# A recurrent mixer and a gated FFN, tile by tile: the FFN's pieces moved to other places in the order, with alternating PSUM banks

## What is computed

```python
xx  = x_prev - x
mix = tanh((x + xx * maa_x) @ maa_w1)          # five mixes of 32: w, k, v, r, g
mw, mk, mv, mr, mg = einsum(mix, maa_w2)
xw, xk, xv, xr, xg = x + xx * (maa_{w,k,v,r,g} + m{w,k,v,r,g})
r, k, v, g = xr @ Wr.T, xk @ Wk.T, xv @ Wv.T, silu(xg @ Wg.T)
decay = exp(-exp(time_decay + tanh(xw @ td_w1) @ td_w2))
# scan over time, state S of 16 heads, 32 x 32 each
y_t = r_t @ (S + u * k_t v_t);   S = decay_t * S + k_t v_t
y = groupnorm(y) * ln_g + ln_b
x1 = layernorm(x + (y * g) @ Wo.T)
h  = gelu(x1 @ ternary(W_fc).T)                # 2048 wide
out = layernorm(x1 + layernorm(h) @ ternary(W_proj).T)
```

## Time and profile before

| what | value |
|---|---|
| median of 3 runs | 3530.97 us |
| the runs | 3509.68, 3533.42 and 3530.97 us |
| the profiled execution | 3509.35 us, of which the span is 3507.2 us and 2.15 us lie around it |
| mean granted TensorE clock in it | 0.983 |
| PE busy | 3143.1 us (90%) |
| DVE busy | 2473.1 us (71%) |
| ACT busy | 1897.2 us (54%) |
| POOL busy | 784.9 us (22%) |

### The profile page before, as it was taken

How to read it: one execution, slowest core, us unless ns; L and a number is a source line. 1 busy time by engine, 2 the same in 40 slices (tenths; PEclk the granted TensorE clock), 3 DMA queues, 4 the chain that set the end, 5 groups by cost and what they waited for, 6 DMA issues and landing times.

```text
span 3507.2 us, 98753 instructions
## 1 busy us (share of the span) xinstructions
PE 3143.1 (90%) x39261; PEld 2257.9 (64%) x39261; DVE 2473.1 (71%) x5108; ACT 1897.2 (54%) x3852; POOL 784.9 (22%) x725
## 2 busy tenths in 40 slices
PE   1899999999999999999999999999999999999997
PEld 0566666766666766666666666766666766666764
DVE  8466686776676676776766776676786776677776
ACT  0445556645566555566555566555566655556653
POOL 3122211122221122221222221222211122221121
PEclk9899999999999999999999999999999999999998
DMA  4000000000000000000000000000000000000000
GB/s 184 14 8 19 20 14 17 17 14 20 14 17 20 17 14 20 14 17 20 17 14 20 14 17 20 17 14 20 14 19 18 17 20 14 20 14 17 20 17 13
DMA packets 22598, 73.04 MB, mean 21 GB/s; under 512 B 3041, under 2 KB 3297, under 8 KB 20545
## 3 DMA queue, kind: packets, MB, share of 16 engines
q1 hardware_dynamic: 22208, 66.76, 5.4%
HBM read 49.97 MB, written 16.78 MB: 19 GB/s over the span
## 4 chain that ended last, share of the span: by engine, by line
PE 25%; DVE 22%; issue 21%; ACT 19%; POOL 10%; POOLq 1%; DMA 1%; ACTq 1%; DVEq 0%; SPq 0%
PE psP L393 7%; ACT ARENA L653 7%; PE psP L423 6%; ACT HHI L810 6%; POOL MT L856 5%; POOL ARENA L870 4%; PE psF L615 4%; ACT GG L801 3%; DVE ARENA L1125 3%; DVE ARENA L1087 3%; DVE ARENA L1077 2%; DVE HLO L1237 2%; DVE SUMS L1229 2%; DVE GR L1245 2%; PE psX L375 1%
## 5 line engine op out<-in xcount | busy, mean ns | idle before, releaser
L393 PE MATMUL psP<-ARENA,WALL 128*128 128x256 f32 x3072 | 692.0, 382 | 0.2 <-ACT ARENA L684 0.2
L653 ACT ACTIVATE ARENA<-ARENA 32x512 f32<-32x512 f32 (+1 forms) x992 | 578.8, 583 | 189.8 <-DVE ARENA L1077 137.7
L393 PEld LDWEIGHTS psP<-ARENA,WALL 128*128 128x128 f32 x3072 | 574.6, 190 | 84.5 <-issue 11.3
L1237 DVE SCALAR_TENSOR_TENSOR HLO<-GG,FWB,HHI 128x128 f16<-128x128 f32 x1024 | 292.3, 347 | 459.8 <-ACT HHI L810 455.7
L615 PE MATMUL psF<-XHI,WFC 128*128 128x128 f16 x4096 | 490.0, 220 | 46.5 <-DVE XLO L1216 34.0
L615 PE MATMUL psF<-XLO,WFC 128*128 128x128 f16 x4096 | 488.8, 220 | 0.0
L615 PEld LDWEIGHTS psF<-XHI,WFC 128*128 128x128 f16 x4096 | 401.7, 99 | 88.1 <-issue 86.0
L615 PEld LDWEIGHTS psF<-XLO,WFC 128*128 128x128 f16 x4096 | 402.9, 98 | 14.0 <-issue 10.3
L870 POOL TENSOR_TENSOR ARENA<-ARENA,XT 128x1024 f32<-128x1024 f32 x128 | 285.2, 2228 | 507.4 <-DVE ARENA L1029 507.4
L634 PE MATMUL psF<-WPJ,HHI 128*128 128x512 f16 x1024 | 389.8, 381 | 3.1 <-ACT GG L801 3.1
L634 PE MATMUL psF<-WPJ,HLO 128*128 128x512 f16 x1024 | 388.1, 379 | 0.0
(11 more groups left out here) (166 smaller groups left out, 5418.0 us busy)
## 6 DMA issues: line engine op xcount, KB each, us to landing
XT<-x_ch SPq DMA_DIRECT2D x33, 520.0 KB, 3.4
ARENA<-x_tok SPq DMA_DIRECT2D x32, 512.0 KB, 4.1
out<-OUT SPq DMA_DIRECT2D x64, 256.0 KB, 2.0
WALL<-w_all SPq DMA_DIRECT2D x5, 1024.0 KB, 16.6
ARENA<-wfc SPq DMA_DIRECT2D x4, 1024.0 KB, 7.9
ARENA<-wpj SPq DMA_DIRECT2D x3, 1024.0 KB, 14.6
GG<-wpj SPq DMA_DIRECT2D x1, 1024.0 KB, 18.6
OUT<-w2a SPq DMA_DIRECT2D x8, 64.0 KB, 14.9
```

Of the source, the lines that this page charges most:

```text
L393: mm = pe.matmul(psP[:, P.bank(f"{name}{g}"), COLS * c:COLS * (c + 1)], WALL[:, w, k, 128 * (2 * g + c):128 * (2 * g + c + 1)], cc(XF[slot ...
L653: return act.activation(o, i, ACT.Copy)
L1237: e = dve.scalar_tensor_tensor(out=HLO[:, k, :], in0=GG[:, u % 2, 0, 128 * m:128 * (m + 1)], scalar=FWB[:, 0, k:k + 1], in1=HHI[:, k, :], ...
```

## The change

Computation and instruction counts stay the same but for four things: each fold of the sums is two TENSOR_REDUCEs of half the size, one SCALAR_TENSOR_TENSOR of 128x1 becomes a TENSOR_SCALAR (the FFN's variance), the names of `XF[0]` and `XF[1]` are swapped for the mixes (so the decay's input no longer shares the gated output's buffer), and the banks of psF follow a table. All else is order:

- VectorE: the last FFN piece `up(1, 3)`, the fold of its sums and `stored` of the first pair go behind the gated output. `late` is cut into `moments` (behind mix "mk"), `product`, `late_normed` and `late_stored`, with mixes and `up(0, 0)` between them. The decay's mix goes behind the first half of the output product. Level 2's right scaling goes in front of `up(0, 3)`, and the first pair's fold goes behind the merges of levels 4 and 8.
- TensorE: mix "mw" between `wo0` and `wo1`; `down(1, 3)` from the body's end to behind td1 of the next body.
- ACT: tanh of the gate's second half behind the second level's query copies. POOL and SP: the late roots and the late store follow VectorE's new order; the same DMAs are issued in the same order.

```diff
+F_BANKS = [0, 1, 0, 1, 0, 1, 1, 0, 1, 0, 1, 0]
 class Ring:
     def bank(self, name):
-        return self.names.index(name) % self.depth
+        return self.banks[self.names.index(name)]
     def wait_free(self, eng, it, name, first):
-        i = self.names.index(name) - self.depth
+        own = self.names.index(name)
+        i = next(i for i in range(own - 1, own - 1 - self.n, -1) if self.banks[i % self.n] == self.banks[own])
...
@@ TensorE
                 mm.then_inc(p_full, 1)
+                if ffn:
+                    ffn.late()
                 mix(it - 1, 2, "mv", wait_free)
...
                     mm.then_inc(p_full, 1)
+                    if p == 0:
+                        mix(it, 0, "mw", wait_free)
                 if ffn:
                     ffn.stats(1)
-                mix(it, 0, "mw", wait_free)
-                if ffn:
-                    ffn.down(1, 3)
...
+                def late():
+                    if not first:
+                        down(before, 1, 3)
@@ ACT
-                    if i == 0:
-                        if ffn:
-                            ffn.up(0, 3)
+                    if i == 0 and ffn:
+                        ffn.up(0, 3)
+                    if i == 1:
                         gate(1)
@@ POOL
-                    v = XF[f % 2].rearrange("p (q t) -> p q t", t=CH)
+                    v = XF[(f + 1) % 2].rearrange("p (q t) -> p q t", t=CH)
                     pool.tensor_tensor(v, v, xcur, ALU.add).then_inc(xf_ready, 1)
-                    if f == 2 and ffn:
+                    if f == 1 and ffn:
                         ffn.late()
...
+                        if ffn:
+                            ffn.late_normed()
@@ VectorE
                 mix(it, 1, "mk", None)
                 if ffn:
+                    ffn.moments()
                     ffn.normalise()
...
                 mix(it, 3, "mr", "k1")
                 if ffn:
+                    ffn.late_normed()
                     ffn.up(0, 0)
+                    ffn.late_stored()
...
                 if ffn:
                     ffn.up(0, 2)
+                scale_right(1, 2)
+                if ffn:
                     ffn.up(0, 3)
                 for i, n in enumerate(LEVELS):
-                    scale(i + 1, n)
+                    if i:
+                        scale_right(i + 1, n)
+                    scale_left(i + 1, n)
...
                     dve.wait_ge(w_dve, W.read(it, f"l{n}"))
-                scale(5, 32, ffn.fold if ffn else None)
+                    if ffn and n in (4, 8):
+                        ffn.fold(0, n // 4 - 1)
+                scale(5, 32)
...
-                if ffn:
-                    ffn.up(1, 3)
-                    ffn.stored()
                 dve.wait_ge(y_copied, 2 * it + 2)
...
                 dve.tensor_tensor(YSB[:, 512:1024], YSB[:, 512:1024], G[:, 512:1024], ALU.mult).then_inc(z_ready, 1)
                 if ffn:
-                    ffn.stats(1)
+                    ffn.up(1, 3)
+                    ffn.fold(1, 0)
+                    ffn.fold(1, 1)
+                    ffn.stored()
...
                     dve.bn_stats(BNS[:, p, :], X1[:, p, :]).then_inc(bn_done, 1)
-                decay_input(it, "wo1")
+                    if p == 0:
+                        decay_input(it)
...
+                def fold(p, i):
+                    dve.wait_ge(sums_added, 3 * (PAIRS * j + p) + 3)
+                    dve.tensor_reduce(GR[:, i, :], SUMS[:, i, :].rearrange("p (m t) -> p t m", m=4), AX.X, ALU.add).then_inc(sums_folded, 1)
```

More of the change, by code:

```diff
@@ L67, in __init__ @@
         self.before = before
+        self.banks = banks or [i % depth for i in range(self.n)]
         assert self.n % depth == 0
     def bank(self, name):
-        return self.names.index(name) % self.depth
+        return self.banks[self.names.index(name)]
     def full(self, it, name):
@@ L91, with __init__ @@
 class FeedForward:
-    def __init__(self, alone, normalise=None, tokens=None, up=None, stats=None, down=None, bias=None, finish=None, normed=None, stored=None, fold=None, late=None):
+    def __init__(self, alone, normalise=None, tokens=None, up=None, stats=None, down=None, bias=None, finish=None, normed=None, stored=None, fold=None, moments=None, late_normed=None, late_stored=None, late=None):
         self.alone, self.tokens, self.up, self.stats, self.down = alone, tokens, up, stats, down
@@ L233, in rwkv_ffn_kernel @@
         X = Ring(X_SEQ, 1, x_full, {"act": x_act, "dve": x_dve})
-        F = Ring(F_SEQ, 2, f_full, {"act": f_act, "stats": f_stats, "product": f_product})
+        F = Ring(F_SEQ, 2, f_full, {"act": f_act, "stats": f_stats, "product": f_product}, banks=F_BANKS)
         xprev, xcur = XT[:, :, 0:CH], XT[:, :, 1:CH + 1]
@@ L638, in alone @@
                 def alone():
+                    late()
                     tokens()
@@ L643, in alone @@
                         for part in range(4):
-                            down(p, part)
+                            down(j, p, part)
                         stats(p)
-                return FeedForward(tokens=tokens, up=up, stats=stats, down=down, alone=alone)
+                def late():
+                    if not first:
+                        down(before, 1, 3)
+                return FeedForward(tokens=tokens, up=up, stats=stats, down=lambda p, part: down(j, p, part), late=late, alone=alone)
             over_tiles(pe, tile, feed_forward)
@@ L923, in late, with late_normed @@
                         scale_root(before, 1)
+                def late_normed():
+                    if not first:
                         out_root(before, 1)
@@ L1079, in scale, with scale_left @@
                         queries(i, 2 * n)
-                    if between:
-                        between()
+                def scale_left(i, n):
+                    tl, tr = TOT[n].rearrange("p (q two) -> p two q", two=2)[:, 0, :], TOT[n].rearrange("p (q two) -> p two q", two=2)[:, 1, :]
                     if i == 0:
@@ L1282, in stored, with finish, late @@
                                       ALU.subtract, ALU.mult).then_inc(out_ready, 1)
-                def late():
+                def finish(j, p):
+                    moments(j, p)
+                    product(j, p)
+                def late(part):
                     if not first:
-                        finish(before, 1)
-                        normed(before, 1)
-                        stored(before, 1)
+                        part(before, 1)
                 def alone():
@@ L1292, in alone @@
                     tokens()
-                    late()
+                    late(moments)
+                    late(product)
+                    late(normed)
+                    late(stored)
                     for p in range(PAIRS):
@@ L1301, in feed_forward @@
                 return FeedForward(normalise=normalise, tokens=tokens, up=up, stats=stats, finish=lambda: finish(j, 0), normed=lambda: normed(j, 0),
-                                   stored=lambda: stored(j, 0), fold=lambda: stats(0), late=late, alone=alone)
+                                   stored=lambda: stored(j, 0), fold=fold, moments=lambda: late(moments), late=lambda: late(product), late_normed=lambda: late(normed), late_stored=lambda: late(stored), alone=alone)
             over_tiles(dve, tile, feed_forward)
```

57 lines of the change are left out of this document (32 added, 25 removed).

## The result

| what | before | after |
|---|---|---|
| median of 4 runs each | 3531.43 us | 3361.94 us (3360.7 to 3363.1) |
| ratio to before | 1 | 0.953, 95% interval 0.9497 to 0.9563 |
| profiled execution: span | 3507.2 us | 3361.0 us, and 2.1 us around it |
| mean granted TensorE clock | 0.983 | 0.993 |

The change takes 4.7% off.

The account below looks back on a forecast made before the run. TensorE bounds the tile, so its waits are the possible gains: 104.12 - 1.8 + 0.2 - 1.1 + 0.5 = 101.9 us a tile, 3415 us in all. Forecast case 3400 to 3435 us, full range 3378 to 3455 us.

Parts of the forecast that it names:

- The gated output, -1.8: Before the output product: gated output comes 1.8 us earlier, leaving TensorE 0.1 us idle in place of 1.88.
- The clock, -1.7 where it was met: Output product: without the idle time it always runs in 7.13 us, not 8.83, saving 1.7 us in slow tiles.
- The decay's input, a wait of 1.0 us from collisions: Before td1: POOL's low mixes delay VectorE, so TensorE waits 1.0 us in place of 0.8; bounds 0.1 and 1.8.
- The low tokens' wait of 1.1 us: Before the FFN: TensorE's wait for its low tokens disappears, minus 1.1 us a tile.
- The ladder, +0.55: Ladder levels: half folds delay level 32, so key transposes start 0.55 us later; from 0.2 to 1.0 us.
- rival 5: Slower: clock falls on the ladder after three waits of 0.8 to 1.0 us; 110.5 us a tile, 3675 us; chance 0.03.
- The down quarter "costs nothing": Behind td1: the down projection's moved last quarter fills TensorE during VectorE's next mix, adding no time.
- The decay's mix priced as +0.2: Before td1: the tile sum adds 0.2 us for a 1.0 us wait for the decay's input in place of 0.8.
- some us that I leave out: Last tile: banks by table let fc0 start before the down product is read; unpriced there, 0 in the loop.
- the collisions miss and the ladder hides its folds: Waits of 0.1 us before td1, 0.2 us on the ladder: 100.6 to 101.2 us a tile, 3373 to 3395 us; chance 0.15.

Follow-up runs that it names:

- the piece alone: Kernel before, with only VectorE's last FFN piece and the stored result moved behind the gated output: 3425.6 us, ratio 0.9705.
- the fillers: Kernel before, with eight unneeded 128x512 matmuls per tile put into TensorE's idle time ahead of the output product: 3479.7 us, ratio 0.986.

## Why the prediction was off

The record forecast 104.12 us to become 101.9. By places on TensorE (the scan's first mask is VectorE's), in a tile of before at full clock, in the tile after from 1588.57 us (its period is 100.72), and in the mean of the 29 periods after (before's last row is the distance to the next product, 1738.62 to 1767.87 us):

| stretch | before | forecast | after, one tile | after, mean |
|---|---|---|---|---|
| output product to td1 | 11.55 | 9.7 | 9.37 | 9.06 |
| td1 to fc0 | 13.88 | 14.7 | 13.94 | 14.10 |
| fc0 to the scan's first mask | 27.1 | 27.1 | 27.13 | 27.13 |
| first mask to the key transposes | 22.33 | 22.9 | 22.81 | 22.83 |
| key transposes to the next product | 29.25 | 27.4 | 27.47 | 27.47 |
| sum | 104.1 | 101.8 | 100.7 | 100.6 |

- **The gated output, -1.8: right.** The last row moved by 1.78 us, and the piece alone gave the same in the kernel before.
- **The clock, -1.7 where it was met: right,** by the fillers, which gave all of it and nothing else. The product's two halves run at full clock, as forecast.
- **The decay's input, a wait of 1.0 us from collisions: wrong.** This step failed. VectorE's addition ends 8.8 us behind the product's start in every tile of the loop, as if there were no POOL, and td1 can start at 8.9: a wait of 0.1 to 0.2 us where nothing else delays it, the forecast's own lower bound. What delays td1 beyond that is the gap at the loop's jump, between nothing and 0.57 us, so that it starts 8.90 to 9.38 us behind the product, 9.06 in the mean. The collisions did take place, with all three instructions that the record named, and the loser was POOL: its pieces took 1.88, 0.81 and 1.69 us for 0.72, VectorE's sum and addition 1.22 and 1.23, as in the kernel before. The record read the loser off, where VectorE's 128x1 operation took 1.31 us behind a POOL addition that had begun 0.88 us before it. Here VectorE had begun first: the last piece of POOL starts 0.14 us behind the addition, and the first one, though 0.07 us ahead of the sum, starts under the FFN instructions in front of the sum, which run until 1589.17 + 1.14 = 1590.31 us. The other order stands in the same trace, in the first tile, where POOL's last piece began 0.17 us before VectorE's addition: there the addition took 1.62 us for 1.23, and the piece kept its 0.72.

```profile
188.06 0.72 POOL L867 TENSOR_TENSOR MT<-TMA,ARENA 32x256 fp32r<-32x256 f32 x1
...
188.23 1.62 DVE L1057 TENSOR_TENSOR ARENA<-ARENA,XT 128x1024 f32<-128x1024 f32 x1
```

  The Trainium skill, "SBUF — State Buffer", section "Who interferes with whom", says that the one who issues first gets the shared ports for the whole instruction and the other blocks. The trace agrees, in both orders; the record took the loser for granted where that rule leaves it to the order. POOL's delay, 8.53 - 6.31 = 2.2 us, costs TensorE nothing, but not by much: its mix for the decay waits for the first two pieces, and the second ends 0.1 us ahead of it (1592.83 and 1592.96 us). The other six are for the mixes of the next body.
- **td1 to fc0: the mechanism right, its size too big by 0.6 us.** The low tokens' wait of 1.1 us has gone. But the down quarter, forecast at 1.9 us, adds 1.56: eight matmuls start 0.22 us apart (1600.56, 1600.79), the next mix starts at 1602.11, 3.43 us behind td1's start where it was 1.87, and a row is longer (0.38 us) than that distance, so that the end of the last one lies under the next row. From the mix of v to td2 it is 0.75 us and was 0.95 (its two products started at 1677.15 and 1677.66 us, 0.51 us apart, where the decay's mix above takes 0.33): some of what the record took for work was waiting. From td2 to fc0 it is another 0.17 us less, for the reason of the quarter: the wait of 1.13 us is counted from the end of k's row, and without a wait fc0 starts 0.17 us ahead of that end. 1.56 - 0.20 - 0.17 - 1.13 is the +0.06 of the one tile; the record had 1.9 - 1.1.
- **Behind td1, a collision that VectorE did lose, and that the record had not priced.** The mean of the second row is 14.10 and not 13.94, since a tile where td1 starts early gains nothing by it. In the tile from 1690.04 us td1 starts 8.90 us behind the product, and then:

```profile
1702.80 2.18 POOL L881 TENSOR_TENSOR ARENA<-ARENA,XT 128x1024 f32<-128x1024 f32 x1 [1.39 <-DVE ARENA L1046]
...
1703.51 1.75 DVE L1243 TENSOR_SCALAR X<-X,MV,RSTD 128x512 f32<-128x512 f32 x1
...
1705.31 0.55 PE L610 MATMUL psW<-CF,X 128*128 128x128 f32 x3
```

  VectorE normalises the FFN's input (L1243). Its first half begins under POOL's addition for k and ends 0.28 us behind it, after 1.75 us; the second half takes 0.53. TensorE's transposes of that input (L610) start 0.05 us later. In all 29 periods the first half ends 15.2 or 15.3 us behind the product, whether it starts 13.5 or 13.9 us behind it, and fc0 starts at 23.12 to 23.32 us. So of a gap of up to 0.57 us at the jump at most 0.2 reach fc0, and to hide the gap gained nothing. What the hold costs is an estimate: 8.90 us, and the 13.94 us of the tile in which TensorE came too late to meet it, give 22.84, and 23.13 was the median, so 0.3 us a tile. No run took it away.
- **The ladder, +0.55: right as a sum (0.48),** and made of +1.04 for the folds and -0.6 for the right scaling, as the two kernels with them taken back show. The record's +0.55 holds 0.63 us for the right scaling, so 1.2 for the folds. It said that larger waits come at levels 16 and 32; they came at 8, 16 and 32, 0.9 to 1.1 us each, and the clock stayed up (rival 5 did not happen).
- **The down quarter "costs nothing": true in the changed kernel** (100.6 us a tile either way) **and not by itself.** With the decay's mix back it is the difference between 3400.7 and 3521.6 us.
- **The decay's mix priced as +0.2** by the wait in front of td1 alone. What the move is worth is what would stand there without it, 1.2 to 5.2 us a tile. The sum came out near since the record compared with the tile before, not part with part.
- **Left out: the two ends.** The stretch ahead of the first full period is 9.8 us shorter (391.43 to 381.67 us), forecast 4. Part of it is the clock: the fillers alone took 5.3 us off it. It is 379.4 us with the banks alone back, so that some 2 us of it stay open. The tail behind the last gated output went from 3507.2 - 3436.53 = 70.7 us to 3361.0 - 3298.77 = 62.2 us. The record says that the banks give "some us that I leave out". By the kernel with the banks back, whose tail is 67.3 us, they are 5.0 of the 8.4.

So the miss of 53 us is 38 us in the loop (29 x 1.3), 6 at the start and 8.4 in the tail. In the loop 0.6 us a tile fall to td1's start, where a wait of 1.0 us was forecast, 0.6 to the stretch behind it, and the rest of 0.1 is rounding.

The rival nearest to the result was the second, "the collisions miss and the ladder hides its folds", 3373 to 3395 us. Its per-tile time (100.6 to 101.2) holds the measured one, and that is luck: the collisions that it says miss did hit and fell on POOL, the ladder hid nothing, and the terms behind td1 made up for it. The rivals varied only two terms, so the tail and the stretch behind td1 had no case that widened the range.

**Open.** Why the clock falls in half, in all or in every second tile for the same idle time is not shown. Nor is it shown by a run what the tile would take if POOL's addition for k did not lengthen VectorE's normalisation, nor what makes the gap at the jump vary from tile to tile.

## What to carry to other kernels

Price a moved piece by what stands in its place when it is gone, and price it together with the filler next to it: here one order of the same work ran at 105.8 us a tile and another at 101.8, since the waits of one order were longer, lay close together and took the clock down. When TensorE has short idle stretches, look at the granted clock behind them before anything else, and try a few filler matmuls: they separate the clock's price from the wait's in one run. Where two engines' instructions exclude each other, ask which one will have begun first before you say which one waits. Read the same stretch in several tiles: a gap of 0.56 us in one was absent in another. And add up work on an engine by the starts of its rows, not by their lengths, and write down the head and the tail of the loop as terms of the sum.

## What the hardware did that I had not expected

- Several short waits can lower the clock together: 1.37, 0.28 and 0.84 us within 4 us took TensorE to 0.50 for some 7 us, while waits of 1.1, 0.9 and 1.0 us on the ladder and behind it, further apart, left it at 1.00. Whether the 1.37 us alone would have done it is not shown.
- The same wait of 1.89 us lowered the clock in 14 of 29 tiles of one kernel, nearly every second one, and in the kernel before in the first half of the profiled execution and not in the second; by the times and clocks of its other executions it was in fewer tiles or in all.
- More work was faster: eight extra matmuls a tile took 50 us off the kernel.
- Between VectorE's two-input instructions and POOL's, the one that had begun later was the longer one. POOL's pieces took 1.88 and 1.69 us for 0.72 beside VectorE's queue without gaps, and VectorE kept its 1.22 us. Where POOL had begun first, VectorE's addition took 1.62 us for 1.23, and its normalisation, a TENSOR_SCALAR, 1.75 for 0.53.
- TensorE lost between nothing and 0.57 us at the loop's jump when nothing was queued for it to finish there.
